# Score products of a masked, padded attention on 32 rows in place of 17

## What is computed

```
gate = sigmoid((token_inputs @ Wg)[..., 0])
_, idx = top_k(gate, C)                      # C = N / 2 = 256 tokens
attn_in = take_along_axis(token_inputs, idx[..., None], axis=1)
q = (attn_in @ Wq).reshape(B, C, H, dh)      # H = 16 heads, dh = 16
k = (attn_in @ Wk).reshape(B, C, H, dh)
v = (attn_in @ Wv).reshape(B, C, H, dh)
scores = einsum('bqhd,bkhd->bhqk', q, k) / sqrt(dh)
attn = softmax(scores, axis=-1)
o = einsum('bhqk,bkhd->bqhd', attn, v).reshape(B, C, D) @ Wo
out = zeros.at[arange(B)[:, None], idx].set(o * gate_sel[..., None])
x = x + out
```

## Time and profile before

| | |
|---|---|
| median of 3 runs | 3720.81 us (3718.06 to 3724.72) |
| span of the profiled execution | 3694.4 us |
| PE busy | 3148.3 us, 85% |
| DVE busy | 2387.3 us, 65% |
| ACT busy | 1268.4 us, 34% |
| select stage with attention | 3228.3 to 3691.5 us of the span |

### The profile page before, as it was taken

The page is one execution under the profiler, slowest core; times in us unless marked ns, Lnnn a source line. Parts: engine busy times, 40 slices in busy tenths (PEclk is TensorE's granted clock), DMA queues, the critical chain, the costliest instruction groups (busy, mean ns, idle before and its releaser), DMA issues. The chain is left out here.

```text
span 3694.4 us, 48384 instructions
## 1 busy us (share of the span) xinstructions
PE 3148.3 (85%) x17898; PEld 2411.9 (65%) x17898; DVE 2387.3 (65%) x5793; ACT 1268.4 (34%) x2457; POOL 173.5 (5%) x165
## 2 busy tenths in 40 slices
PE   5999947889999999955889889898989888488887
PEld 2655534444899999933676767777677778355654
DVE  6787524554677777775577878686767764354442
ACT  2333202221344444422434443434434431133332
POOL 0000000006111111100000000000000000000000
PEclk8999967999999999977778979797969875678886
DMA  1000080003699999952011111111101100100000
GB/s 64 23 12 18 12 154 23 12 18 126 235 321 321 320 321 316 318 201 85 24 35 35 38 33 58 41 38 35 38 32 38 35 15 1 61 12 24 12 18 12
DMA packets 203646, 326.80 MB, mean 88 GB/s; under 512 B 37449, under 2 KB 157522, under 8 KB 202258
## 3 DMA queue, kind: packets, MB, share of 16 engines
q1 hardware_dynamic: 196930, 305.94, 25.2%
q0 software_dynamic: 6480, 17.77, 1.3%
HBM read 275.15 MB, written 48.50 MB: 88 GB/s over the span
## 5 line engine op out<-in xcount | busy, mean ns | idle before, releaser
L767 PE MATMUL ex_ps<-ex_xbT,ex_w 128*128 128x128 f32 x4544 | 530.6, 275 | 0.5 <-issue 0.5
L767 PEld LDWEIGHTS ex_ps<-ex_xbT,ex_w 128*128 128x128 f32 x4544 | 524.1, 192 | 4.5 <-issue 0.7
L1386 PE MATMUL de_ps<-de_hT,de_w 128*128 128x512 f32 x640 | 329.7, 662 | 23.1 <-DMA de_w<-in_w_kqv_dram 18.1
L896 ACT ACTIVATE ex_t<-ex_ps,ex_b 128x128 f32<-128x128 f32 x568 | 208.8, 368 | 334.8 <-PE ex_ps L767 318.0
L711 PE MATMUL ex_ps<-ex_xT,ex_w 128*128 128x512 f32 x512 | 230.1, 606 | 12.4 <-DVE ex_gl L1008 9.1
L1386 PEld LDWEIGHTS de_ps<-de_hT,de_w 128*128 128x128 f32 x640 | 129.0, 212 | 157.0 <-issue 149.4
L1008 DVE SCALAR_TENSOR_TENSOR ex_gl<-ex_ps,ex_b,ex_t 128x128 f32<-128x128 f32 (+1 forms) x316 | 123.6, 391 | 137.1 <-ACT ex_t L896 68.3
L711 PEld LDWEIGHTS ex_ps<-ex_xT,ex_w 128*128 128x128 f32 x512 | 97.9, 194 | 131.9 <-issue 115.1
L1571 PE MATMUL de_ps<-de_qx,de_kx 128*128 128x128 f32 x512 | 89.4, 346 | 98.4 <-ACT de_qx L1638 98.4
L1814 DVE SCALAR_TENSOR_TENSOR de_ya<-de_kx,de_taps,de_ya 128x512 f32<-128x512 f32 x192 | 143.4, 749 | 15.7 <-ACT de_ya L1626 11.2
L1814 DVE SCALAR_TENSOR_TENSOR de_ya<-de_qx,de_taps,de_ya 128x512 f32<-128x512 f32 x192 | 141.3, 750 | 18.9 <-ACT de_ya L1626 14.1
(11 more groups left out here) (377 smaller groups left out, 6071.7 us busy)
## 6 DMA issues: line engine op xcount, KB each, us to landing
ex_w<-in_w_all_dram SPq DMA_DIRECT2D x144, 1024.0 KB, 6.4
ex_w<-in_w_all_dram SPq DMA_DIRECT2D x72, 512.0 KB, 8.7
de_w<-in_w_kqv_dram SPq DMA_DIRECT2D x80, 256.0 KB, 3.1
de_ab<-alpha_d SPq DMA_DIRECT2D x8, 2048.0 KB, 7.4
ex_xb<-ex_xs_d SPq DMA_DIRECT2D x71, 129.0 KB
ex_xs_d<-ex_blank SPq DMA_DIRECT2D x71, 128.5 KB, 8.6
ex_w<-ex_y_d SPq DMA_DIRECT2D x16, 512.0 KB, 6.1
mx_xin<-in_x_dram SPq DMA_DIRECT2D x8, 512.0 KB, 3.9
```

The lines of the kernel that those rows point to most:

```text
L767: m = pe.matmul(ps[:, n % 4, x * BLK:(x + 1) * BLK], w[:, k, part * HID + c * P:part * HID + (c + 1) * P], xbT[sx][:, k, :], start=(k == 0 ...
L896: act.activation(t1[:, n % 2, 0:BLK], ps[:, n % 4, 0:BLK], ACT.Identity, bias=b13[s][:, 0, n:n + 1]).then_inc(t1_ready, 1)
L1386: m = pe.matmul(ps[:, n % 2, :], w[:, g % SLOTS, k, n % 2 * P:(n % 2 + 1) * P], hT[:, k, :], start=(k == 0), stop=(k == KT - 1))
```

## The change

The slice of rows that both score products use goes from 17 rows (row 0 and the 16 of the head) to the whole tile of 32. The constant that held 17 goes. The added rows are zero in `qT`, `kT` and `q2`. Each engine has the same instructions in the same order as before; what differs is the number of rows in the two operands of the 1024 records of L2144 and L2161, and that all lines behind the removed one are numbered one lower.

```diff
@@ -2051,7 +2051,6 @@
     PAD = 32
     QUAD = P // PAD
     NQ = H // QUAD
-    KROWS = DH + 1
     SCALE = DH ** -0.5
     ctx = ExitStack()
     own = []
@@ -2105,7 +2104,7 @@
         block = ctx.enter_context(nc.Block())
         tok = lambda x, b: x[b].rearrange("(t p) d -> p t d", p=P)
         steps = [(b - 1 if b else None, b if b < BATCH else None) for b in range(BATCH + 1)]
-        rows = lambda i: slice(i * PAD, i * PAD + KROWS)
+        rows = lambda i: slice(i * PAD, (i + 1) * PAD)
 
         @block.sync
         def _(sp):
```

## The result

| | before | changed |
|---|---|---|
| median | 3719.43 us (6 runs, 3710.68 to 3724.72) | 3688.68 us (6 runs, 3661.32 to 3692.58) |
| ratio | | 0.9906, 95% interval 0.9878 to 0.9934 |
| span of the profiled execution | 3694.4 us | 3685.7 us |
| attention part of select (first score product to the end) | 466.3 us | 434.6 us |

A forecast was written before the change was run, and what follows sets the result against it. TensorE was taken to bound the select stage, with 20.5 us of each 58.00 us step at half clock. Seven steps 27.8 plus last step 3.8 gave 31.6 us: 3720.8 to 3689 us, range 3670 to 3709.

The forecast's parts named there:

- No direct cost: Both score products: a product's time goes by its columns, so 32 rows in place of 17 cost 0.
- slower rival: Score blocks: full tiles keep neighbours from overlapping, up to 164 us lost, 3771 us at half the overlap; chance 0.04.
- The clock follows the rows: TensorE in select: the clock follows array rows fed over time, whatever their values; 3689 us (3672 to 3709), chance 0.79.
- Term (a): Stretch ahead of the selection product (L2201): clock comes back, product runs wholly at the higher level, 1.44 us a step.
- Term (b): Second low period, at the Q projection: scores, values and L2217 at the higher level, 3.34 us a step, else only 1.46.
- Term (c): First clock fall of the step, at 3411.51: stays, as rows don't fill the waits for VectorE and ScalarE; no gain.
- Term (d): The seven steps: stretches fall elsewhere in each, four win 4.78 us and three 2.90, together 27.8 us.
- Term (e): Last step: slow nearly throughout, each block followed by a VectorE wait; two of four score and value pairs regained, 3.8 us.
- upper bound: All blocks of the low periods at the higher level: 6.66 us a step, 56.4 us together with the last step.
- The sum against the time: Whole time: median 3720.8 us lies 26.4 above the 3694.4 span, taken as around the span; span after 3662.8, time 3689.
- busy time alone decides: Rival on TensorE's clock: only busy time counts, so time stays 3721 us; one reading of the no-change case, chance 0.13.
- the clock holds throughout: Rival, select stage: even the first fall goes, saving nears 56.4 us, time 3664 to 3672; chance 0.04.

The follow-up runs named there:

- with three places: Filler products, read by nobody, ahead of three of TensorE's waits for VectorE's maxima, on the kernel before (17 rows): attention part 443.0 us; on 32 rows 411.7.
- with more: Those fillers plus three ahead of group 1's scores and four ahead of each group's maxima in the last step: attention part 422.1 us (17 rows), 405.6 (32).

## Why the prediction was right, step by step

**No direct cost: right.** The blocks take the same at equal level. On PE's timeline, the turned scores with 17 rows at the higher and the lower level:

```profile
3428.54 1.16 PE L2161 MATMUL se_ps<-se_q,se_kT 17*128 17x256 f32 x16 [0.51 <-DVE se_q L2384]
3435.34 2.11 PE L2161 MATMUL se_ps<-se_q,se_kT 17*128 17x256 f32 x16 [0.51 <-DVE se_q L2384]
```

and with 32 rows, the lower level first:

```profile
3428.56 2.11 PE L2160 MATMUL se_ps<-se_q,se_kT 32*128 32x256 f32 x16 [0.51 <-DVE se_q L2383]
3439.16 1.16 PE L2160 MATMUL se_ps<-se_q,se_kT 32*128 32x256 f32 x16 [0.51 <-DVE se_q L2383]
```

So the slower rival, that whole tiles would no longer overlap, has no part in the result.

**The clock follows the rows: right.** It is 0.79, 0.84 and 0.89 over the attention part with 17, 24 and 32 rows, with no other difference in the program. The doubt that zero rows may not count is settled: they do count, and ones beside them count no more. The clocks named ahead came too: 0.91 in the seven steps and 0.73 in the last. The rows that led to the forecast did not separate rows from all else: the 64-row products that left the clock low also have 64 columns each, where the 128-row ones that raised it have 512. Only the runs with 17, 24 and 32 rows do.

**Term (a), the selection product, 1.44 us a step: right**, 5.09 to 3.65. **Term (b), 3.34 us in four steps of seven: the size was low.** The whole of it came in the steady step: 2.11 - 1.16, 1.86 - 1.00 and 5.11 - 3.65, together 3.27, and all steady steps are alike. **Term (c), that the first fall stays: half right.** It stayed but comes later and is half as long, 6.83 us for 13.65. What the forecast did not have is the new period of 3.41 us at the gate product (PE's wait just ahead of it is the same in both kernels, 1.90 and 1.91 us, so that wait alone doesn't bring it), which goes from 1.72 to 3.08 us in the chain; with the scores behind it (1.09 to 1.35) it takes back 1.62 us a step. So the two errors nearly cancel: 1.44 + 3.27, less 1.62, and 0.42 won by L2143 (2.22 to 1.80), gives 3.51, against 58.00 - 54.6 = 3.4 measured. For seven steps the forecast had 27.8 us; the runs gave 405.1 - 379.2 = 25.9. **Term (d), four steps better than three others: wrong.** All steady steps take 54.6 us. **Term (e), the last step, 3.8 us from two pairs of scores and values: low, and from the wrong blocks.** It went from 61.2 us (3633.2 to the end of the span) to 55.4, 5.8 less. Nor is each of its blocks followed by a wait for VectorE, as the forecast read it: in the kernel before, the turned scores, values and next scores of a group run on end from 3647.48 to 3653.67 us, and only then PE waits, 2.25 us ahead of the turned maxima. The changed kernel's last step on PE's timeline:

```profile
3635.35 2.11 PE L2160 MATMUL se_ps<-se_q,se_kT 32*128 32x256 f32 x16 [0.51 <-DVE se_q L2383]
...
3644.30 2.11 PE L2160 MATMUL se_ps<-se_q,se_kT 32*128 32x256 f32 x16 [0.51 <-DVE se_q L2383]
...
3653.20 2.11 PE L2160 MATMUL se_ps<-se_q,se_kT 32*128 32x256 f32 x16 [0.51 <-DVE se_q L2383]
...
3662.59 2.11 PE L2160 MATMUL se_ps<-se_q,se_kT 32*128 32x256 f32 x16 [0.52 <-DVE se_q L2383]
...
3676.96 3.72 PE L2254 MATMUL se_ps<-se_o,se_pselT 128*128 128x256 f32 x16 [0.69 <-ACT se_o L2341]
```

All four turned scores still run at the lower level. What came back is the spread back, 5.96 to 3.72 us, which the forecast had in its upper bound alone, and parts of other blocks behind the scores.

**The sum, 31.6 us; measured 31.7 in the attention part and 30.8 between the medians.** That it agrees so closely is in part chance: (b) and (e) were too small, and the new period at the gate product was missing. The single runs of the changed kernel also spread over 31 us, as much as the whole gain. The upper bound holds up better as a number by itself: a step without any lower level was put at 58.0 - 6.66 = 51.3 us, and the kernels with fillers on 32 rows take 51.4.

**The sum against the time: wrong in one point.** The 26.4 us between span and median were put down as lying around the span. Only 1.8 of them do, by the spans of the single runs; the rest fits the short delta stage of the profiled execution, 23.6 us under that of the changed kernel's. So the span forecast, 3662.8, was not met (3685.7), though the time was.

**Rivals.** That busy time alone decides falls: 17, 24 and 32 rows with the same 2449 products give three clocks. TensorE's busy share of the attention part even goes down as the clock goes up, from 82% at 17 rows to 80% at 32, and with 17 rows and fillers it is 87% at a clock of only 0.86. That the clock holds throughout did not happen with rows alone; it took fillers.

## What to carry to other kernels

Cut a stage with many short waits by the granted clock before looking for slow instructions: here 20.5 us of a 58 us step ran at half clock though TensorE was busy for 18.4 of them. Products that use part of a row tile can be given the whole tile, with zeros in the added rows of both operands, at no cost in their own time and with a gain in the clock. Where TensorE waits for another engine anyway, products that nobody reads, sized to end before the wait does, gave as much again (0.982 of the time before, against 0.990), and a gain in one stretch has to be looked for over the whole step, as the low period can come back elsewhere.

## What the runs showed of the hardware that was not expected

The length of a steady step takes few values. It is 58.0 us with 17 rows and with 32 rows in the turned product alone; 54.6 with 24 rows, with 32 in the first product alone, with 32 in both and with ones in K; 51.4 with fillers on 32 rows, where no lower level is left in the step. At 54.6 the time at the lower level still differs, 13.7 us a step with 24 rows and 10.2 with 32, and the length does not. So a small gain in the clock can leave a step as long as it was, and another be worth 3.4 us; what makes the lengths come out so was not tested. Fillers on 17 rows gave unequal steps instead, 51.8 to 56.8 us with three places and 51.4 to 57.0 with more.

The delta stage, unchanged in all kernels, takes 1459 to 1484 us from one profile to another, 530 to 594 us of it at the lower level by the clock records of the traces. In the profiles of the kernels before and after it is 538 us of 1460 and 589 of 1484: 51 us more at half clock, for 24 us more time. The spread between the runs of one kernel may come from there. The whole runs point the same way, the changed kernel's shortest with a span of 3659.5 us at a mean clock of 0.870 and its longest with 3690.8 at 0.864, but in which stage they differ was not measured.
